# Softmax ahead of the former batch's halves, one memory load per batch, and row transfers issued by ScalarE, in a gated cross-attention kernel

## The reference

```python
memory_proj = einsum('bme,de->bmd', memory, W_mem)
scores = einsum('bnd,bmd->bnm', x, memory_proj) / sqrt(512)
attn = softmax(scores)
memory_context = einsum('bnm,bmd->bnd', attn, memory_proj)
gate = sigmoid(einsum('bnf,df->bnd', concatenate([x, memory_context]), W_gate) + b_gate)
fused = x + gate * memory_context
out = fused * rsqrt(mean(square(fused)) + 1e-6) * norm_w
```

## Time and profile before

| what | value |
|---|---|
| median of 3 runs | 334.95 us (334.11 to 336.81) |
| the profiled execution | 332.4 us, of it the span of instructions 330.2 us |
| busy share of the span | PE 87%, DVE 66%, ACT 52%, POOL 51% |
| mean granted TensorE clock | 0.947 of full speed |
| chain that ended last, by engine | PE 30%, DVE 20%, SP's issues 13%, DMA 13%, ACT 10% |
| DMA | 61.40 MB, mean 186 GB/s |

### The profile page before, as it was taken

One profiled execution on the slowest core, in us unless ns is written; L12 is line 12 of the kernel. 1 busy time (PEld: TensorE's weight loads), 2 busy tenths in 40 slices (PEclk: granted clock), 3 DMA queues, 4 the chain that ended last, 5 costly groups with the idle time before them and its releaser, 6 DMA issues.

```text
span 330.2 us, 4795 instructions
## 1 busy us (share of the span) xinstructions
PE 285.8 (87%) x1479; PEld 243.6 (74%) x1479; DVE 216.5 (66%) x388; ACT 171.7 (52%) x363; POOL 169.7 (51%) x135
## 2 busy tenths in 40 slices
PE   8999699899995499999997499999998499996392
PEld 4979488778884498788886498788887398884362
DVE  4995556677676536877577626777777736786344
ACT  5865354457544537456555546546555445553412
POOL 1244248555655544665658544665758543653302
PEclk9999979999999599999999599999999699999787
DMA  7959953757766293866846383766837464652411
GB/s 285 423 152 240 284 185 85 240 187 248 212 186 191 53 276 101 263 201 177 281 136 199 110 267 111 233 207 188 277 92 232 138 199 113 201 147 52 155 48 65
DMA packets 57048, 61.40 MB, mean 186 GB/s; under 512 B 39104, under 2 KB 39360, under 8 KB 56768
## 3 DMA queue, kind: packets, MB, share of 16 engines
q1 hardware_dynamic: 57024, 61.10, 60.6%
HBM read 43.25 MB, written 7.34 MB: 153 GB/s over the span
## 4 chain that ended last, share of the span: by engine, by line
PE 30%; DVE 20%; SPq 13%; DMA 13%; ACT 10%; issue 7%; POOL 5%; DVEq 0%; POOLq 0%
SPq L262 7%; DMA pT_raw<-blocks_p 6%; DVE pT_lo L694 6%; DMA mem_raw<-in_mem 6%; PE gate_ps L347 5%; PE gate_ps L349 4%; PE gate_ps L354 4%; SPq L269 4%; POOL memT_lo L878 3%; DVE work L743 3%; ACT work L593 2%; DVE top L706 2%; DVE work L737 2%; PE score_ps L347 2%; ACT probs L566 2%
## 5 line engine op out<-in xcount | busy, mean ns | idle before, releaser
L878 POOL TENSOR_TENSOR mem_lo<-mem_raw,mem_hi 128x768 fp32r<-128x768 f32 x32 | 68.1, 2129 | 23.4 <-ACT mem_hi L537 23.4
L878 POOL TENSOR_TENSOR memT_lo<-memT_raw,memT_hi 128x752 fp32r<-128x752 f32 x31 | 56.6, 1825 | 30.0 <-ACT memT_hi L537 30.0
L896 POOL TENSOR_TENSOR guarded<-meansq,eps 128x1 f32<-128x1 f32 x27 | 5.1, 190 | 98.7 <-ACT work L588 98.7
L566 ACT ACTIVATE probs<-score_ps,shift 112x375 f32<-112x375 f32 x32 | 18.3, 573 | 56.8 <-DVE shift L708 56.8
L728 DVE STREAM_TRANSPOSE blocks_am<-am 128x256 f32<-128x256 f32 x32 | 14.3, 446 | 42.0 <-ACT am L579 38.8
L694 DVE TENSOR_TENSOR pT_lo<-pT_raw,pT_hi 128x384 fp32r<-128x384 f32 x32 | 33.0, 1031 | 11.6 <-ACT pT_hi L537 11.6
L758 DVE SCALAR_TENSOR_TENSOR work<-work,rstd,norm_w 128x512 f32<-128x512 f32 (+1 forms) x29 | 39.8, 1375 | 1.1 <-POOL rstd L931 1.0
L593 ACT ACTIVATE work<-work 128x512 f32<-128x512 f32 (+1 forms) x29 | 17.8, 616 | 36.3 <-DVE work L737 36.3
L743 DVE SCALAR_TENSOR_TENSOR work<-work,ctx_ps 128x512 f32<-128x512 f32 (+1 forms) x28 | 19.0, 679 | 23.9 <-ACT work L593 22.0
L537 ACT ACTIVATE mem_hi<-mem_raw 128x768 fp32r<-128x768 f32 x32 | 26.9, 840 | 13.7 <-DMA mem_raw<-in_mem 13.7
L347 PE MATMUL gate_ps<-wgx_hi,xT_hi 128*128 128x512 f32 x108 | 32.0, 422 | 0.1
(11 more groups left out here) (125 smaller groups left out, 665.0 us busy)
## 6 DMA issues: line engine op xcount, KB each, us to landing
mem_raw<-in_mem SPq DMA_DIRECT2D x32, 384.0 KB, 4.1
memT_raw<-in_memT SPq DMA_DIRECT2D x32, 376.0 KB, 3.5
x_rows<-in_x SPq DMA_DIRECT2D x28, 256.0 KB, 4.5
out<-work SPq DMA_DIRECT2D x27, 256.0 KB, 4.7
pT_raw<-blocks_p SPq DMA_DIRECT2D x128, 48.0 KB, 2.5
xT_raw<-in_xT SPq DMA_DIRECT2D x7, 640.0 KB, 6.3
amT_raw<-blocks_am SPq DMA_DIRECT2D x128, 32.0 KB, 1.9
xT_raw<-in_xT SPq DMA_DIRECT2D x3, 512.0 KB, 5.8
```

The lines of the kernel that those rows point to most:

```text
L566: act.activation(probs[0:ROWS, 0:KEYS], scores[:, 0:KEYS], ACT.Exp, bias=shift[:, n % 2:n % 2 + 1], scale=D ** -0.5, accum_out=total[:, n ...
L878: return pool.tensor_tensor(out, in_, high.bitcast(F32), ALU.subtract)
```

## The change

- One load brings memT and mem of a batch together (`load_mems`), from a joined DRAM array, into one of three slots; the third slot is `first_raw`, which the opening has finished with. It is issued in step s for batch s + 2. Before, memT was issued for s + 3 and mem for s + 1. The first three batches are still loaded in two parts, and the opening's weights wmT land in `work`.
- blocks_p and pT_raw have two buffers each, with one semaphore each; pT_hi and pT_lo lie in wgc_hi, whose weights are used up after the opening.
- ACT: exponentials(s) comes ahead of pT_high(s - 1). DVE: pT_low(s - 1) comes behind maximum, fuse, turn_p and shares.
- The factor 512^-0.5 is put into q when its halves are made (ACT's copy with a scale, DVE's subtraction with a product), so that the maximum is negated within its own instruction, and the shift instruction and `top` are gone.
- x rows and output tiles are issued by ACT: load_x behind square, the store one step later than before, ahead of square. SP keeps the stores of the last two tiles.

```diff
+MEMS = MEMT + MEM
+RAW = 3
...
-        memT_raw = sb("memT_raw", [P, 2, MEMT])
-        mem_raw = sb("mem_raw", [P, 2, MEM])
+        mems_raw = sb("mems_raw", [P, 2, MEMS])
...
-        blocks_p = sb("blocks_p", [P, KPAD])
-        pT_raw = sb("pT_raw", [P, KPAD])
-        pT_hi, pT_lo = (sb(f"pT_{s}", [P, 2, KC, P], F32R) for s in ("hi", "lo"))
+        blocks_p = sb("blocks_p", [P, 2, KPAD])
+        pT_raw = sb("pT_raw", [P, 2, KPAD])
...
+        raws = [mems_raw[:, 0], mems_raw[:, 1], first_raw[:]]
...
+        pT_hi, pT_lo = (wgc_hi[:].rearrange("p c d -> p (c d)")[:, i * 2 * KPAD:(i + 1) * 2 * KPAD].rearrange(
+            "p (s c n) -> p s c n", s=2, c=KC) for i in range(2))
...
+            def load_mems(n):
+                sp.wait_ge(memT_lo_ready, n - RAW + 1)
+                sp.wait_ge(mem_lo_ready, n - RAW + 1)
+                sp.dma_start(raws[n % RAW], mems_d[n]).then_inc(mems_loaded[n % RAW], 16)
 
             def move_p(n):
                 sp.wait_ge(blocks_p_ready, n + 1)
-                if n >= 1:
-                    sp.wait_ge(pT_lo_ready, n)
+                if n >= 2:
+                    sp.wait_ge(pT_lo_ready, n - 1)
...
-            def finish(tile):
-                sp.wait_ge(h_ready, tile + 1)
-                if tile + X_SLOTS < ALL_TILES:
-                    load_x(tile + X_SLOTS)
-                sp.wait_ge(y_ready, tile + 1)
-                sp.dma_start(out_d[tile], y[:, tile % 2]).then_inc(y_stored[tile % 2], 16)
...
-                if s + 3 < BATCHES:
-                    load_memT(s + 3)
-                if s + 1 < BATCHES:
-                    load_mem(s + 1)
+                if s + 2 < BATCHES:
+                    load_mems(s + 2)
                 if x_load_at(s) is not None:
                     load_xT(*x_load_at(s))
-                if tile_at(s - 1) is not None:
-                    finish(tile_at(s - 1))
...
-                high(qT_hi[:, half, c:c + w], banks[n % 2][:, 0:w]).then_inc(q_hi_ready, 1)
+                act.activation(qT_hi[:, half, c:c + w], banks[n % 2][:, 0:w], ACT.Copy,
+                               scale=D ** -0.5).then_inc(q_hi_ready, 1)
...
+            def load_x(tile):
+                act.wait_ge(h_ready, tile - X_SLOTS + 1)
+                act.dma_start(x_rows[:, tile % X_SLOTS], x_d[tile]).then_inc(x_loaded[tile % X_SLOTS], 16)
+
+            def store(tile):
+                act.wait_ge(y_ready, tile + 1)
+                act.dma_start(out_d[tile], y[:, tile % 2]).then_inc(y_stored[tile % 2], 16)
...
-                if s - 1 < BATCHES:
-                    pT_high(s - 1)
                 if late:
                     split_memT(s + 1)
                 for n in softmaxes_at(s)[:1]:
                     exponentials(n)
+                if s - 1 < BATCHES:
+                    pT_high(s - 1)
                 if s - 2 < BATCHES:
                     amT_high(s - 2)
+                if tile_at(s - 2) is not None:
+                    store(tile_at(s - 2))
                 if before is not None:
                     square(before)
+                    if before + X_SLOTS < ALL_TILES:
+                        load_x(before + X_SLOTS)
...
-                dve.tensor_reduce(top[:, s], scores[:, 0:KEYS], AX.X, ALU.max).then_inc(top_ready, 1)
-                dve.wait_ge(top_ready, n + 1)
-                dve.tensor_scalar(shift[:, s], top[:, s], -D ** -0.5, None, ALU.mult).then_inc(shift_ready, 1)
+                dve.tensor_reduce(shift[:, s], scores[:, 0:KEYS], AX.X, ALU.max, negate=True).then_inc(shift_ready, 1)
...
-                if s - 1 < BATCHES:
-                    pT_low(s - 1)
                 for n in softmaxes_at(s)[:1]:
                     maximum(n)
                 if before is not None:
                     fuse(before)
                 for n in softmaxes_at(s)[:1]:
                     turn_p(n)
                     shares(n)
+                if s - 1 < BATCHES:
+                    pT_low(s - 1)
```

More of the change, by code:

```diff
@@ L150, in build_gated_cross_attention @@
         eps = sb("eps", [P, 1])
-        zeros = blocks_p[:, 0:D // 2].bitcast(BF16)
+        zeros = blocks_p[:, 0, 0:D // 2].bitcast(BF16)
         def raw_of(unit, first=0, end=DC):
@@ L171, in build_gated_cross_attention @@
         probs_blocks = probs[:].rearrange("p (c j r) -> p c j r", j=Q, r=R)
[L172 to L175, removed]
+        blocks_ps = [blocks_p[:, i] for i in range(2)]
+        pT_raws = [pT_raw[:, i] for i in range(2)]
+        turned_p = [a.rearrange("p (j c r) -> p c j r", j=Q, r=R) for a in blocks_ps]
+        pT_flat = [a.rearrange("p (q n) -> p q n", q=Q) for a in pT_raws]
+        pT_rows = [a.rearrange("p (q c r) -> p c q r", q=Q, r=R) for a in pT_raws]
+        blocks_p_rows = [[a[R * q:R * (q + 1)].rearrange("p (j n) -> p j n", j=Q) for q in range(Q)] for a in blocks_ps]
         blocks_am_rows = [blocks_am[R * q:R * (q + 1)].rearrange("p (j n) -> p j n", j=Q) for q in range(Q)]
@@ L308, in _ @@
             move_am(0)
-            load_memT(4)
+            load_mems(3)
             move_p(2)
@@ L315, in _ @@
             move_am(1)
-            load_memT(5)
-            load_mem(3)
+            load_mems(4)
             for s in range(OPENING, STEPS):
@@ L721, in pT_low @@
                 dve.wait_ge(pT_hi_ready, n + 1)
-                low(pT_slot(pT_lo, n), pT_rows, pT_slot(pT_hi, n)).then_inc(pT_lo_ready, 1)
+                low(pT_slot(pT_lo, n), pT_rows[n % 2], pT_slot(pT_hi, n)).then_inc(pT_lo_ready, 1)
             def turn_am(n):
@@ L800, in _ @@
             dve.wait_ge(memT_hi_ready, 1)
-            low(memT_lo[:, 0], memT_raws[:, 0], memT_hi[:, 0]).then_inc(memT_lo_ready, 1)
+            low(memT_lo[:, 0], memT_raws[0], memT_hi[:, 0]).then_inc(memT_lo_ready, 1)
             q_low(0, 1, 0)
@@ L886, in split_memT @@
                 pool.wait_ge(memT_hi_ready, n + 1)
-                low(memT_lo[:, n % 2], memT_raws[:, n % 2], memT_hi[:, n % 2]).then_inc(memT_lo_ready, 1)
+                low(memT_lo[:, n % 2], memT_raws[n % RAW], memT_hi[:, n % 2]).then_inc(memT_lo_ready, 1)
             def split_mem(n):
                 pool.wait_ge(mem_hi_ready, n + 1)
-                low(mem_lo[:, n % 2], mem_raws[:, n % 2], mem_hi[:, n % 2]).then_inc(mem_lo_ready, 1)
+                low(mem_lo[:, n % 2], mem_raws[n % RAW], mem_hi[:, n % 2]).then_inc(mem_lo_ready, 1)
             def inverse_rms(t):
@@ L967 @@
         "xT": xT,
-        "memT": chunked(memT).reshape(BATCHES, P, MEMT),
-        "mem": chunked(turned_rows(padded(memory, 1, KPAD))).reshape(BATCHES, P, MEM),
+        "mems": np.concatenate([chunked(memT).reshape(BATCHES, P, MEMT),
+                                chunked(turned_rows(padded(memory, 1, KPAD))).reshape(BATCHES, P, MEM)], axis=2),
         "first": np.concatenate([chunked(w_memT.T).reshape(P, 2, DC // 2 * E),
```

78 lines of the change are left out of this document (40 added, 38 removed).

## The result

| kernel | median | lowest to highest | span in the profile |
|---|---|---|---|
| before | 335.11 us | 334.11 to 336.81 | 330.2 us |
| changed | 341.40 us | 340.36 to 342.52 | 338.9 us |

The change makes the kernel slower: the ratio is 1.018, with an interval of 1.013 to 1.024. The forecast was 322. What came is the rival on the other side, the load of mem and memT as the new bound. The spans are of one execution each, of 332.4 us before and 340.7 changed. The one before was 2.7 us under its median, so the spans differ by 8.7 us where the medians differ by 6.3.

The account below looks back on a forecast made before the run. TensorE was taken as the bound, with idle gaps to win. Terms -8.1 - 0.9 + 1.5 - 4.5 + 0.4 - 1.6 = -13.2 took 332.4 to 319.2, and 322 as a median; 8-in-10 range 313 to 336.

Parts of the forecast that it names:

- the rival on the other side: Load becomes the bound: memT_hi waits for the joint load in every step; about 343 us, chance 0.15.
- The loop: Each step, memT_hi through turn_am and SP's issues to the load's landing: 4.3 + D, 8.6 us; +0.4 in all.
- D: Time of the joint 760 KB load until landing, not in the trace; taken as 4.3 us, between 3.5 and 6.3.
- break-even of 9.4: Old mean step (75.00/8), from which the load becomes the bound: 4.3 + D = 9.4, so D = 5.1.
- The opening: Before the loop: keeps its order but for one load, 0 us.
- The order of the halves: Steps 10, 18, 26 with what led into them: -8.1 us; steps 5, 13, 21: -0.9; steps 8, 16, 24: +1.5.
- the clock rival: Clock holds at 2.4 GHz in steps 11, 19, 27: 1.4 us more each; 315 or less, chance 0.05.
- The lock: DVE beside POOL's xT_lo: stall moves from pT_lo to fuse; -0.3 us each in steps 5, 13, 21.
- The end: Last batches: load for batch 31 issued in step 29, not behind move_p(31); -4.5 us.
- The issuers: x loads and stores on ACT: SP's relief -1.6 us in the first group, ACT's cost 0.
- ACT held: ACT held by its issues: 1 us more in steps 10, 18, 26, six light steps and the end; 328, chance 0.14.
- Double buffers and scale: Scale in q, double buffers of blocks_p and pT_raw, pT_hi in wgc_hi: 0 us.

Follow-up runs that it names:

- e3: The changed kernel with x loads and stores issued by SP again, at the end of its step; 344.17 us.
- e7: The changed kernel with the joint load cut in two at the same place and for the same batch, memT issued first; 322.98 us.
- e11: The changed kernel with the joint load cut in two at the same place, mem issued first in the loop; 340.24 us.
- e1: The changed kernel with memT (for s + 3) and mem (for s + 2) as two loads into the three slots, opening's memT earlier too; 316.17 us.
- e9: The changed kernel with only its opening mended: memT(3) and memT(4) loaded by themselves and early, joint load kept in the loop; 337.13 us.
- e8: The kernel before with only the order of the halves changed: exponentials ahead of pT_high, maximum and fuse ahead of pT_low; 326.82 us.
- e5: The kernel of e1 with the old order of the halves; 319.55 us.
- e12: The kernel of e1 with mem loaded for s + 1 instead of s + 2, memT staying at s + 3; 320.48 us.
- e6: The kernel of e1 with x loads and stores issued by SP again; 316.88 us.
- e2: The changed kernel with the joint load kept but issued ahead of move_am(s - 1), in the opening too; 325.72 us.

## Why the prediction was wrong

**The loop was seen, and its turn was sized too short.** The prediction wrote it as 4.3 + D with D = 4.3, so 8.6. D is about 5.0, above the 4.7 that the prediction had worked out for the pair. The choice was the failing step: "I take 4.3, nearer the pair, as x and store no longer ride behind it". They matter little: with them on SP again D is 5.1 and 5.3 in the two rows, against 5.1 and 4.8 (e3). What counts is that memT cannot be used before the last byte of mem has landed. As a transfer of its own, first at the same place, memT lands after 3.6 (e7), and 18.4 us come back.

**The fixed part was short too.** It came from step 14, a clean full step, where ACT, DVE and SP were all free. In the eight turns above, from memT_hi to the load's issue, it is 4.3, 5.0, 4.3, 4.9, 4.3, 4.3, 4.5 and 4.8, 4.55 in the mean. In the turn of 5.0 (9.90 - 4.88) it is SP's queue: move_p, late by a locked fuse, stands in front of move_am. So with D at 5.0 the turn is 9.3 to 10.0, at the break-even of 9.4 or over it, and 9.6 in the mean. e11 shows the same: at D = 4.7 the old formula gives 9.0, under the full step, and the kernel still takes 340.2.

**It was held against the wrong thing.** The prediction compared the turn with each kind of step by itself and charged the light steps 0.1 each. But the loop turns once for each batch, so it is to be held against the mean step of a group. In e1 that mean is 72.9 / 8 = 9.1 us and 9.0 in the next piece: this is the bound once the order of the halves has made steps 10 and 18 shorter, not the 9.4 of before, and the gain of those steps can't be had by a kernel whose loop takes 9.4 or more. The break-even of 9.4 was right only for "no loss"; for the forecast gain the turn had to be under 9.1, so D under 4.8 with the fixed part of 4.3, and under 4.5 or so with one of 4.55. The assumed 4.3 would have passed even so; the measured 5.0 does not.

**The opening was costed at nothing.** "The opening keeps its order but for one load: 0" is wrong. In the kernel before memT(3) and memT(4) are issued ahead of move_p(1) and move_p(2); in the changed kernel they come with the two joint loads, and the first of these stands behind move_am(0). ACT's timeline, and SP's for the load's issue, show what that costs:

```profile
34.65 0.83 ACT L533 ACTIVATE memT_hi<-mems_raw 128x752 fp32r<-128x752 f32 x1 [5.72 <-DMA mems_raw<-in_mems]
```

```profile
29.80 0.53 SPq L263 DMA_DIRECT2D mems_raw<-in_mems  x1
```

score(3) starts 4.8 us later, and e9 gets 4.3 back. A moved load has to be followed in every place where it is issued, not in the loop alone.

**The order of the halves: right alone, too much in the sum.** The chain of a step without a tile was put at 6.8; it is 6.8, 6.8 and 6.9 in e1 and 7.0 in e8. The whole part was put at -8.1 - 0.9 + 1.5 = -7.5, and e8, alone, has -8.0 by the medians, and -7.3 by the two profiles from score(3) on. But with the rest of the change and early loads the order is worth only 3.4 (e1 against e5). The prediction gave mem's earlier load nothing in steps 10, 18 and 26, and e5 shows that it, or another part of the rest, wins some of the same microseconds; the terms were added as if they were apart. That e1 comes out below 322 all the same is no proof of the terms: it has some 4 us that no term foresaw (below). Part of the gain is given back at once, while the clock is low: score(11) to score(12) takes 13.3 us in e1 and 12.6 before. The rows still hold, so the clock rival is out: in e1 the first group of score(11) lasts 0.94 where 0.51 is the time at 2.4 GHz.

**The lock: right in kind.** By the rule of the Trainium skill (SBUF — State Buffer, "SBUF: two separate sides") the lock goes to fuse, and the trace agrees: fuse takes 2.26, 2.28 and 2.48 us in steps 10, 13 and 16 of the changed kernel, and pT_lo, now behind it, 0.53. Rows of DVE, then of POOL, in step 13:

```profile
138.22 2.28 DVE L763 SCALAR_TENSOR_TENSOR work<-work,x_rows 128x512 f32<-128x512 f32 x1
...
140.95 0.53 DVE L708 TENSOR_TENSOR wgc_hi<-pT_raw,wgc_hi 128x384 fp32r<-128x384 f32 x1
```

```profile
137.54 2.40 POOL L891 TENSOR_TENSOR xT_lo<-xT_raw,xT_hi 128x1024 fp32r<-128x1024 f32 x1
```

Its price depended on the load. Steps 8, 16 and 24 were to cost 0.5 each. They cost 1.6 to 2.1 more than before in the changed kernel (11.1 to 11.5 us), 0.0 to 0.5 in e8, and nothing in e1 (9.4). Steps 5, 13 and 21 gained 0.6 to 0.7 each in e1, not 0.3.

**The end: right in size, hidden by the load.** The term was -4.5 and e12 prices it at 4.3, with early memT. In the changed kernel it was not seen, as memT_hi(31) itself waits 4.34 us for the joint load, issued 4.6 us earlier:

```profile
306.19 0.83 ACT L533 ACTIVATE memT_hi<-mems_raw 128x752 fp32r<-128x752 f32 x1 [4.34 <-DMA mems_raw<-in_mems]
```

The exponentials behind it start 6.6 us after score(30), forecast 6.9; attend(31) comes 21.0 after it, forecast 18.4, and TensorE ran at the low clock on the way, for some 3 us from 301 and again from 308 (the granted clock is 0.69 in the mean of 301 to 310).

**The issuers: right in sign.** SP's relief was put at 1.6 and ACT's cost at 0; by the medians the two together are worth 0.7 (e6) and 2.8 (e3), and neither is clear of the spread. Nowhere does ACT lose by its issues: undoing them never made the kernel faster. The rule of the Trainium skill that spoke against it (DMA: Bandwidth & Descriptors, "Issuing engines are not separate DMA queues") says that only issue time is saved, and the runs agree as far as the loads of SP go: 20 of the 29 joint loads land after 5.1 with either issuer, the other nine 0.5 sooner with two. The other one (Perfetto Trace Analysis, "DMA Instruction — HWDGE") would have had ACT held for up to an issue of SP. In e2 22 issues of ACT overlap one of SP; ACT's take 0.34 to 0.56 us and SP's 0.54 to 0.62, against 0.34 to 0.47 and mostly 0.54 to 0.61 in the changed kernel, where all but two are apart. So the rival "ACT held" falls.

**Double buffers and scale: 0 was too little.** e12 is e8 with these, with three slots for the loads instead of two, with wgc_hi for pT_hi and pT_lo, with the changed kernel's other edits to the opening, and with ACT as issuer: 320.5 against 326.8. The issuer explains perhaps 0.7. By the starts of the scores 1.7 of the 6.4 us between the two spans lie ahead of score(3); that is the late start told of under e8, and no gain of an edit. 1.9 lie behind score(31). So some 4 us are not told apart. Which of the edits brings them wasn't tried; the third slot, which lets a load be issued while the two former batches are still in use, is one of them.

**The sum.** Forecast 322; e1, the change with memT's lead kept, takes 316.2. So the difference of 25.2 us between e1 and the changed kernel is the load alone: about 4.3 in the opening (e9), and the rest in the loop and at the end. That the load rival's own number, 343, came so close to 341.4 is luck. It had D = 5.7 and turns of 10.0, so 15 us more in three groups, less 6.5 for mem's lead. Measured are turns of 9.6 and 1.5 us more in the three pieces, the end included; the other 7.2 us lie ahead of score(9), where the rival had nothing. The chance of 0.15 for the load rival was too low: one of the two nearest rows for D, the xT load, was over its break-even, and the formula's other term had been read in the best of all steps.

## What to carry to other kernels

- When two transfers are joined, each gets the landing time of both together, and their leads become one. Here the join, at the same place and for the same batch, cost 18 us in 341 against two loads with memT in front, and only 1 against two with mem in front. Ask of each half when it was used, and follow the loop that its issue is now in.
- Sum up such a loop from its worst steps too, where the queues in front are full, and hold its mean turn against the mean step. A break-even within 20% of a guessed term is a coin toss and should be priced like one.
- Put the transfer that is used first in front of its large neighbour, and a small one that something waits for in front of both.

## What the runs showed of the hardware

- An issue by ACT occupies its queue for 0.34 to 0.35 us (43 of the 50 in the changed kernel, the longest 0.47) and runs beside ACT's own instruction. Both rows start within 0.02 us of each other:

```profile
109.61 0.57 ACT L566 ACTIVATE probs<-score_ps,shift 112x375 f32<-112x375 f32 x1 [1.33 <-DVE shift L721]
109.63 0.34 ACTq L603 DMA_DIRECT2D out<-work  x1
```

- The transfers that ACT issues stand in a DMA queue of their own (q10 in the profile), and land sooner than the same ones from SP: 3.9 and 4.1 us in the changed kernel for x rows and stores, 5.3 and 5.6 in e3. Their place in time differs too, for in e3 they follow the joint load at once, so the runs don't tell the queue from the place: in e2 ACT's land after 2.9 and 2.1.
- The landing of a load grows more slowly than its size: 376 KB 3.6 us, 760 KB 5.1 (4.7 in e2, where it is issued elsewhere). A small transfer behind the large one pays for it: 1.9 to 3.4 us for 32 KB pieces.
- Now and then an issue of SP is stretched, from 0.54 us to 1.69 for the load at 126.61 in the changed kernel. The kernel before has such rows too (1.34 at 122.41), with no second issuer, and one issue of ACT in e1 takes 1.24 (at 165.18). The runs don't say why.
